# One-hot comparisons for four fields by one instruction, in two larger buffers

## What is computed

```python
B, F, E, UNITS = 2048, 39, 64, 128
e = jnp.stack([tbl_0[ids[:, 0]], ..., tbl_38[ids[:, 38]]], axis=1)   # (B, F, E)
delta = jnp.einsum('uf,bfe->bue', inner_w, e)
z = jnp.sum(delta * delta, axis=-1)                                  # (B, 128)
h = jnp.concatenate([z, dense_ctx], axis=1)
h = jnp.maximum(h @ W_top1 + b_top1, 0.0)
h = jnp.maximum(h @ W_top2 + b_top2, 0.0)
y = h @ W_top3
```

## Time and profile before

| | us |
|---|---|
| median of 3 runs | 967.73 |
| lowest, highest | 964.75, 969.58 |
| span of the profiled execution | 600.5 |
| difference of the median to that span | 367.2 |
| PE busy, its weight loads | 493.2, 472.8 |
| POOL, DVE, ACT busy | 418.1, 434.2, 256.5 |

### The profile page before, as it was taken

One profiled execution on the slowest core, in us unless ns is written; L12 is line 12 of the kernel. 1 busy time (PEld: TensorE's weight loads), 2 busy tenths in 40 slices (PEclk: granted clock), 3 DMA queues, 4 the chain that ended last, 5 costly groups with the idle time before them and its releaser, 6 DMA issues.

```text
span 600.5 us, 11038 instructions
## 1 busy us (share of the span) xinstructions
PE 493.2 (82%) x4000; PEld 472.8 (79%) x4000; DVE 434.2 (72%) x821; ACT 256.5 (43%) x314; POOL 418.1 (70%) x407
## 2 busy tenths in 40 slices
PE   0045489994999699998999599987999539999997
PEld 0035489894999689988999599987999539999995
DVE  4159959984878668775888579774888519787782
ACT  1175334361545244353536244352535214455763
POOL 6777677777777777777777777777777777772000
PEclk9998789996999879997999889996999859999999
DMA  3783765211631166113731177113531851110000
GB/s 69 141 199 97 98 124 103 38 25 45 92 64 23 24 77 98 27 26 50 90 61 25 24 79 95 24 27 46 93 62 30 84 82 25 25 25 10 2 2 0
DMA packets 35560, 35.00 MB, mean 58 GB/s; under 512 B 10816, under 2 KB 27203, under 8 KB 35497
## 3 DMA queue, kind: packets, MB, share of 16 engines
q1 hardware_dynamic: 22696, 21.18, 23.2%
q0 software_dynamic: 12800, 13.13, 12.0%
q10 hardware_dynamic: 16, 0.01, 0.0%
HBM read 34.28 MB, written 0.01 MB: 57 GB/s over the span
## 4 chain that ended last, share of the span: by engine, by line
POOL 50%; PE 18%; issue 17%; DVE 5%; DMA 4%; SPq 3%; ACT 1%; POOLq 0%
POOL x_all L304 50%; PE side L346 4%; PE turned L390 3%; SPq L263 3%; PE delta L406 3%; PE delta L407 3%; PE delta L408 3%; DMA x_all<-tbl 2%; DMA x_all<-tbl,idx 2%; DVE onehot L563 2%; PE side L370 2%; DVE table L634 1%; PE side L362 1%; DVE x_all L631 1%; DVE x_all L576 1%
## 5 line engine op out<-in xcount | busy, mean ns | idle before, releaser
L304 POOL DMA_INDIRECT x_all<-tbl,idx x400 | 417.4, 1043 | 125.9 <-issue 121.4
L346 PE MATMUL side<-table,onehot 125*128 125x192 bf16 x1856 | 180.4, 259 | 54.1 <-DVE table L634 37.8
L346 PEld LDWEIGHTS side<-table,onehot 125*128 125x128 bf16 x1856 | 166.9, 105 | 60.4 <-issue 37.8
L584 DVE TENSOR_TENSOR acc_all<-acc_all,sq 128x1024 f32<-128x1024 f32 x120 | 147.3, 1227 | 57.8 <-ACT sq L479 57.3
L479 ACT ACTIVATE sq<-delta 128x1024 f32<-128x1024 f32 x120 | 123.0, 1025 | 129.7 <-PE delta L408 128.3
L406 PE MATMUL delta<-xh,wjh 117*128 117x256 f32 x512 | 155.0, 303 | 4.5 <-issue 4.5
L563 DVE TENSOR_SCALAR onehot<-idh,row_no 125x512 bf16<-125x512 f16 x464 | 144.4, 381 | 7.6 <-ACT idh L458 7.4
L407 PE MATMUL delta<-xl,wjh 117*128 117x256 f32 x512 | 145.9, 285 | 0.0
L408 PE MATMUL delta<-xh,wjl 117*128 117x256 f32 x512 | 145.9, 285 | 0.0
L390 PE MATMUL turned<-ident,x_all 128*117 128x128 f32 x352 | 92.2, 394 | 45.4 <-DMA x_all<-tbl,idx 44.9
L390 PEld LDWEIGHTS turned<-ident,x_all 128*117 128x117 f32 x352 | 83.8, 314 | 47.0 <-issue 46.2
(11 more groups left out here) (36 smaller groups left out, 129.4 us busy)
## 6 DMA issues: line engine op xcount, KB each, us to landing
idb<-ids_by_field SPq DMA_DIRECT2D x9, 1120.0 KB
x_all<-tbl,idx POOLq DMA_INDIRECT x400
idb<-ids_by_field SPq DMA_DIRECT2D x9, 448.0 KB
x_all<-tbl SPq DMA_DIRECT2D x12, 224.0 KB
idb<-ids_by_field SPq DMA_DIRECT2D x9, 130.0 KB
x_all<-tbl SPq DMA_DIRECT2D x2, 280.0 KB
w2s<-W_top SPq DMA_DIRECT2D x1, 512.0 KB, 22.9
idb<-ids_by_field SPq DMA_DIRECT2D x9, 52.0 KB
```

The source lines that it names most:

```text
L304: pool.indirect_dma_start(x_slots[k][:, f, 0:E], None, tables[f], bass.IndirectOffsetOnAxis(idx[k][:, f:f + 1], 0),).then_inc(gathered[k], 16)
L346: mm = pe.matmul(side[n % 2][:, q * PARTS * E:(q + 1) * PARTS * E], onehot[k % OHR][:, c, q, h * TB:(h + 1) * TB], table[k][:, q, c, :, :] ...
L584: dve.tensor_tensor(acc[p][:, :], acc[p][:, :], sq[(quad - 1) % SQ][:, :], ALU.add).then_inc(summed, 1)
```

## The change

The pairs are put in four groups: (0, 1), (2, 3), (4, 5) and (6). One comparison covers all fields of a group: four fields and 1024 columns in the first three, two fields and 512 columns in the last. A step has 24 wide and 10 narrow comparisons. The ring of three buffers becomes two, each large enough for 8 chunks of 4 fields; groups 0 and 2 use one, 1 and 3 the other. The comparisons of a group are due when those of its first pair were: -3.6, 4.3, 9.3 and 12.8. `hot` counts groups instead of pairs, and a group waits until both pairs of the last user of its buffer are looked up. Matmuls read the same columns in a new layout.

```diff
-OHR = 3
+GROUPS = [(0, 1), (2, 3), (4, 5), (6,)]
+GROUP_OF = {k: g for g, pairs in enumerate(GROUPS) for k in pairs}
...
-HOT_AT = [at - HOT_LEAD for kind, what, at in JOBS if kind == "look" and what[1] == 0]
+HOT_AT = [at - HOT_LEAD for kind, what, at in JOBS if kind == "look" and what[1] == 0 and what[0] in [g[0] for g in GROUPS]]
...
-        onehot = [sb(f"onehot{k}", [KP, MAX_CH, 2, NB], BF16) for k in range(OHR)]
+        onehot = [sb(f"onehot{k}", [KP, 8 * 4 * NB], BF16) for k in range(2)]
+        hot_of = [onehot[g % 2][:, 0:PAIR_CH[pairs[0]] * 2 * len(pairs) * NB]
+                  .rearrange("p (c q b) -> p c q b", c=PAIR_CH[pairs[0]], b=NB) for g, pairs in enumerate(GROUPS)]
...
-                        pe.wait_ge(hot, at_pairs(s) + k + 1)
+                        pe.wait_ge(hot, at_groups(s) + GROUP_OF[k] + 1)
...
-                                           onehot[k % OHR][:, c, q, h * TB:(h + 1) * TB],
+                                           hot_of[GROUP_OF[k]][:, c, 2 * (k - GROUPS[GROUP_OF[k]][0]) + q, h * TB:(h + 1) * TB],
...
-                def make_hot(s, k):
-
-                    dve.wait_ge(cast, (s + 1) * 2 + (1 if 2 * k + 2 <= HALVES[0].stop else 2))
-
-                    if k >= OHR:
-                        dve.wait_ge(looked, at_looks(s) + 2 * (k - OHR) + 2)
+                def make_hot(s, g):
+
+                    pairs = GROUPS[g]
+                    fields = slice(2 * pairs[0], 2 * pairs[-1] + 2)
+                    dve.wait_ge(cast, (s + 1) * 2 + (1 if fields.stop <= HALVES[0].stop else 2))
+
+                    if g >= 2:
+                        dve.wait_ge(looked, at_looks(s) + 2 * GROUPS[g - 2][-1] + 2)
                     elif not (isinstance(s, int) and s == -1):
-                        dve.wait_ge(looked, at_looks(s - 1) + 2 * last_in_ring(PAIRS, OHR, k) + 2)
-                    ch = PAIR_CH[k]
+                        dve.wait_ge(looked, at_looks(s - 1) + 2 * GROUPS[g + 2][-1] + 2)
+                    ch = PAIR_CH[pairs[0]]
                     for c in range(ch):
-                        ins = dve.tensor_scalar(onehot[k % OHR][:, c, :, :], idh[:, 2 * k:2 * k + 2, :],
+                        ins = dve.tensor_scalar(hot_of[g][:, c, :, :], idh[:, fields, :],
                                                 row_no[ch][:, c:c + 1], None, ALU.is_equal)
                     ins.then_inc(hot, 1)
...
                 make_hot(-1, 0)
-                make_hot(-1, 1)
...
                         fill_first(k - 2)
-                        if k < PAIRS:
-                            make_hot(-1, k)
+                    if k in (1, 3, 5):
+                        make_hot(-1, (k + 1) // 2)
```

More of the change, by code:

```diff
@@ L221, in build @@
         at_looks = lambda s: (s + 1) * LOOKS
-        at_pairs = lambda s: (s + 1) * PAIRS
+        at_groups = lambda s: (s + 1) * len(GROUPS)
         at_mlps = lambda s: (s - 1) * 4
@@ L456, in cast_ids @@
                     if half == 0:
-                        wait(act, hot, at_pairs(s - 1))
+                        wait(act, hot, at_groups(s - 1))
                     act.activation(idh[:, fields, :], idb[:, fields, :], ACT.Copy).then_inc(cast, 1)
@@ L597, in rows @@
                         todo += [(at + FILL_LAG, "fill", n) for n, (kind, _, at) in enumerate(JOBS) if kind == "look"]
-                        todo += [(HOT_AT[k], "make hot", k) for k in range(PAIRS)]
+                        todo += [(HOT_AT[g], "make hot", g) for g in range(len(GROUPS))]
                     return todo
```

## The result

| | us |
|---|---|
| before, median of 4 runs | 966.24 |
| after, median of 4 runs | 917.4 (910.51 to 922.27) |
| ratio, 95% interval | 0.9496 [0.9425, 0.9568] |
| after, its profiled run and its span | 913.74, 912.0 |

The change makes the kernel 5% faster. Forecast were 972.2 us and a range from 963.5 to 980.0: the time fell by 49 us where I had it rise by 4.5.

What follows compares the result with a forecast made beforehand. It took POOL's gather rounds 1 to 5 and their start to bound the kernel: +6.5 us for five rounds and -2.0 us at the start, +4.5 on 967.73, made 972.2 us, range 963.5 to 980.

Steps and rivals of the forecast that it cites:

- What bounds the kernel: Whole kernel: POOL's rounds 1 to 5 and the first's start set the end; each us there is a us of the end.
- the last one of the sum: Final step: 367.2 us of the median above the profiled span of 600.5 us, left unchanged and added to the forecast.
- waits for nobody in between: POOL's 50 gathers a step: run without waits for other engines, a period of 66.3 to 67.8 us.
- The width: DVE's comparison of 1024 columns: takes 0.48 us, with a start each 0.40 us.
- Rival 4: DVE's wide comparison is not fast, twice 0.34 us: 974 us; its chance is counted in rival 1's.
- The longer hold: Gathers in POOL's rounds: wide comparisons hold the port longer, +1.0 us a round, bounds nothing to 1.9 us.
- the adds: DVE's adds in POOL's rounds: they meet other gathers, +0.3 us a round, bounds -1.5 and +2.
- The rule of the lock: DVE and POOL's shared port: whoever comes second is blocked for the other's whole instruction, which speaks against the change.
- DVE's 4 us a step: DVE's comparisons in a step: 4 us saved against 18.0 us now, worth nothing by itself.
- The start: Before round 1: last table split falls at 69 to 71 us, round 1 starts earlier, 2.0 us won.
- Rival 2: POOL's rounds and start: gathers slip through or are spared, -6 us, 962 us; chance 0.13 for over 0.5% faster.
- rival 1: DVE and POOL's port costs more: +13 us, 981 us, or 976 us with one part only; chance 0.42 in all.

Runs made afterwards that it cites:

- e1: The kernel before, unchanged, profiled anew; 969.77 us, with a span of 968.0 us.
- e15: The kernel before with five short iotas on POOL behind every gather; 749.2 us, ratio 0.7803.
- e16: The changed kernel with five short iotas on POOL behind every gather; 757.89 us, ratio 0.791.
- e5: The changed kernel with a one-element DVE memset ahead of each wide comparison; 949.96 us, ratio 0.9764.
- e8: The kernel before, but its steps compare only chunks 0, 2, 4 and 6 of 8-chunk pairs, 34 comparisons a step; 953.28 us, ratio 0.9834.
- e7: The changed kernel with wide comparisons only ahead of the first step and narrow ones in all steps; 950.40 us, ratio 0.9863.
- e13: The kernel before with three short iotas on POOL behind every gather; 773.04 us (735.59 to 845.54).
- e14: The changed kernel with three short iotas on POOL behind every gather; 777.97 us (714.19 to 810.33).
- e9: The changed kernel, but in rounds 2 to 7 POOL gathers in bursts of five, each further burst waiting for one more unit transposed by PE; 813.12 us, ratio 0.8406.

## Why the prediction was wrong, point by point

- *What bounds the kernel.* The step that failed is the last one of the sum: "the profile does not show that part, and I leave it as it is". I took 367.2 us for something outside the program. The runs show it inside the program: e1's span is 968.0 us of its 969.77, with PE, DVE and ACT stalled while POOL gathers and POOL then waiting for PE, and the earlier trace rows were of an execution in which this did not happen. A gap of 38% between a span and the median says that the profile shows another course of events; no price read in it could be carried over. In the same way POOL, which "waits for nobody in between", turned out to have 308.5 us of waits for PE in e1.
- *The width.* Taken at 0.48 us, measured 0.481. Rival 4 is out.
- *The longer hold.* Taken at +1.0 to +1.3 us a round over 4.9. Where nothing stalls it is +1.1 us a round from round 1 to round 7 (e15 against e16). In ordinary executions gathers are held 3.8 us a round in after and 1.7 in e1 (rounds 2 to 7), +2.1. The sum was right, its parts were not: I had given +1.0 us to the comparisons' own hold and +0.3 to the adds, and over rounds 2 to 7 of e15 and e16 it is +0.2 for gathers that overlap comparisons alone and +1.4 for those that overlap an add or subtraction. The sign of its effect was wrong too: POOL stands 51 us a round anyway (e1), so the hold costs nothing, and beside it the stall of the others comes some 8 us later (round 3). That the 25 us of the steps come from that is argued from these rows and from e5; no run held a few gathers early in a round by other means.
- *The rule of the lock.* The Trainium skill ("SBUF — State Buffer", "Who interferes with whom") has whoever comes second blocked for the other's whole instruction, and I read it as speaking against the change. The trace agrees with the blocking where a gather meets an add (2.32 us, to 0.82 us after the add's end); inside wide comparisons gathers took only 0.99 and 1.28 us. That a hold is good for the kernel follows from the stall alone, which is not in that rule. On its inference that an add of two SBUF tensors should not delay descriptor generation the prediction said too much: adds do hold gathers here, but no row tells the reading of the indices from the generation of descriptors.
- *DVE's 4 us a step.* "Worth nothing by itself": right. e8 saves more of DVE's busy time against e1 (42 us) than after does (27 us) and gets 13 us; e5 loses half of the gain with nearly the same busy time as after.
- *The start.* Taken at -2.0 us, with the last split at 69 to 71. In after it ends at 69.7 us, as worked out, but round 1 starts only at 79.6, when POOL is through with round 0: that takes 76.4 us, where the execution of the earlier trace rows took 68.8 and I had added 0 to 1.3. And the start to compare with is e1's 101.7, not the earlier trace rows's 74.75: in e1 the stall is there from 41 us on (DVE stands 15.4 and 14.9 us before two fills), in after only from about 74. In e15 and e16, which do not stall, it is -1.0 us. e7 shows that wide comparisons ahead of the first step bring the earlier start; that they do it by holding gathers is in line with theory G and was not tried by itself.
- *The rivals.* None had this mechanism. Rival 2 named the right side and the wrong reason (gathers spared). With e15 and e16 in hand, slower by some 1%, between my forecast and rival 1, is the outcome of the same edit in a kernel whose gathers are paced by five iotas.

What stays open: what it is in the chip that backs up. PE's pieces of two and three matmuls each 0.70 us, the stall of three engines at once, and the end of it after a pause of 3.29 us look like something shared that POOL's gathers fill and that drains at its own rate; this is a guess. The Trainium skill ("NOTIFIC — the notification-queue block", section 7.1 on overflow) states that this block's internal pipeline always applies backpressure rather than lose a record. That would look like this; no run here shows whether it is that, and none tells why the execution of the earlier trace rows was spared. If it were that, the stall would belong to the recording: every timed run here lists its span and granted clock and so was recorded, and no run shows whether the stall, and with it the 5% and the 28%, is there when nothing is recorded.

## What to carry to other kernels

Compare the span with the median first: if they differ by more than a few us, take another profile before pricing anything. Where POOL issues indirect DMAs back to back, look whether the other engines have idle time that is put down to "issue"; if so, try to slow POOL down (short instructions behind each gather, waits on what the others have done) before tuning anything else: five iotas brought 22% here, three with the waits 28%, and the tuned comparisons 5%, most likely by doing the same by chance. And see what a change is worth once the stall is away: the wide comparison is a loss of 1.2% where five iotas pace the gathers.

## What I had not expected of the hardware

- While POOL issues gathers of 128 rows each 1.25 us, PE falls from 101 matmuls in 12 us to 48 in the 52 us after (e1, round 3), and ACT and DVE with it; at 1.44 us it does so in some rounds (e13, e14), at 1.60 us in none. One execution, that of the earlier trace rows, did not do it at 1.25 us.
- One pause of 2.8 to 3.7 us in POOL's stream gives PE back its rate, in each of e9's six paced rounds.
- A comparison of 125x1024 bf16 takes 481 ns with its columns in line and 3044 ns in strides of 256, and a row of eight of those held one gather for some 21 us.
- The granted clock follows the stalls: 1.00, its upper level of 2.4 GHz, in the first 12 us of e1's round 3, where PE is busy 11.55 us, and 0.50, the lower of 1.2 GHz, from 352 to 391 us, where PE is busy 9.13 us of 39.
